# Two graph layers with residual norms on one core: the first row block of the adjacency product interleaved with making h

## What is computed

```
h  = item @ W_item.T + b_item
x1 = layernorm(x + relu(adj @ h + x @ W_user.T + b_user))
Wh = x1 @ W
e  = leaky_relu(Wh @ a[:D] + (Wh @ a[D:]).T, 0.2)
x2 = layernorm(x1 + elu(softmax(where(adj > 0, e, -9e15), axis=1) @ Wh))
```

## Time and profile before

| | |
|---|---|
| median of three runs | 2807.78 us (2807.31 to 2808.75) |
| the profiled execution, its own time | 2806.64 us |
| its span | 2804.9 us |
| TensorE (PE) busy | 2757.1 us, 98% |
| VectorE (DVE) busy | 2427.5 us, 87% |
| ScalarE (ACT) busy | 898.5 us, 32% |
| chain that ended last | PE 96%, DMA 2%, DVE 1% |
| HBM read and written | 443.85 MB and 23.55 MB |

### The profile page before, as it was taken

The page is one execution under the profiler, slowest core; times in us unless marked ns, Lnnn a source line. Parts: engine busy times, 40 slices in busy tenths (PEclk is TensorE's granted clock), DMA queues, the critical chain, the costliest instruction groups (busy, mean ns, idle before and its releaser), DMA issues.

```text
span 2804.9 us, 22893 instructions
## 1 busy us (share of the span) xinstructions
PE 2757.1 (98%) x7034; PEld 1291.7 (46%) x7034; DVE 2427.5 (87%) x2634; ACT 898.5 (32%) x730; POOL 3.5 (0%) x33
## 2 busy tenths in 40 slices
PE   7999999999999999999989999999999999999997
PEld 5444444444444444444544444444444444444454
DVE  3888888888888888888889898989898989898987
ACT  2555555555555555555550010101010101010111
POOL 0000000000000000000000000000000000000000
PEclk9999999999999999999999999999999999999999
DMA  9999999999999999999890000000000001010000
GB/s 240 326 310 324 301 312 314 311 311 312 313 313 314 310 315 310 316 308 323 257 242 0 19 15 19 16 19 15 19 16 18 27 7 34 0 34 0 16 8 14
DMA packets 309589, 468.18 MB, mean 167 GB/s; under 512 B 17176, under 2 KB 144152, under 8 KB 309400
## 3 DMA queue, kind: packets, MB, share of 16 engines
q1 hardware_dynamic: 171304, 239.32, 29.7%
q10 hardware_dynamic: 138224, 228.15, 26.8%
HBM read 443.85 MB, written 23.55 MB: 167 GB/s over the span
## 4 chain that ended last, share of the span: by engine, by line
PE 96%; DMA 2%; DVE 1%; issue 0%; ACTq 0%; ACT 0%; SPq 0%; DVEq 0%
PE bank L514 46%; PE bank L554 24%; PE bank L555 23%; DMA area_r<-in_adj_dram 1%; PE bank L512 1%; PE bank L486 1%; PE bank L542 1%; DMA area_p<-in_L_gnn_item_feat_dram 1%; DVE adj_t L598 0%; PE bank L502 0%; PE bank L462 0%; ACTq L292 0%; DMA s_scratch<-ts_row 0%; PE bank L454 0%; DMA b_user_col<-in_L_gnn_b_user_dram 0%
## 5 line engine op out<-in xcount | busy, mean ns | idle before, releaser
L514 PE MATMUL bank<-adj_t,area_h 128*128 128x512 f32 (+1 forms) x3160 | 1338.7, 583 | 1.7 <-DVE adj_t L598 1.7
L598 DVE STREAM_TRANSPOSE adj_t<-area_r 128x2048 f32<-128x2048 f32 (+3 forms) x400 | 893.1, 2233 | 198.2 <-PE bank L514 100.8
L842 DVE SCALAR_TENSOR_TENSOR adj_t<-area_r,c_col,area_h 128x1024 f32<-128x1024 uint8 (+2 forms) x790 | 953.9, 1255 | 105.6 <-PE bank L555 104.3
L514 PEld LDWEIGHTS bank<-adj_t,area_h 128*128 128x128 f32 x3160 | 597.7, 191 | 706.1 <-issue 696.9
L944 ACT ACTIVATE mask_out<-adj_t 128x4096 uint8<-128x4096 f32 (+1 forms) x200 | 700.1, 3501 | 640.0 <-DVE packing L666 371.0
L554 PE MATMUL bank<-adj_t,area_r 128*128 128x512 f32 x1580 | 808.9, 594 | 9.0 <-DVE adj_t L842 9.0
L555 PE MATMUL bank<-adj_t,area_r 128*128 128x512 f32 (+1 forms) x1580 | 776.5, 573 | 0.0
L555 PEld LDWEIGHTS bank<-adj_t,area_r 128*128 128x128 f32 x1580 | 301.4, 191 | 377.8 <-issue 377.8
L554 PEld LDWEIGHTS bank<-adj_t,area_r 128*128 128x128 f32 x1580 | 300.3, 191 | 350.6 <-issue 323.0
L775 DVE TENSOR_TENSOR area_h<-area_p,bit_of 128x2048 uint32<-128x2048 uint32 (+1 forms) x100 | 220.8, 2208 | 0.0
L1077 ACT COPY area_h<-bank 128x512 f32<-128x512 f32 x10 | 5.8, 585 | 469.3 <-PE bank L555 469.3
(11 more groups left out here) (123 smaller groups left out, 485.2 us busy)
## 6 DMA issues: line engine op xcount, KB each, us to landing
area_r<-in_adj_dram SPq DMA_DIRECT2D x312, 512.0 KB, 10.7
area_r<-in_adj_dram ACTq DMA_DIRECT2D x312, 512.0 KB, 11.0
area_r<-in_adj_dram SPq DMA_DIRECT2D x78, 480.0 KB, 8.9
area_r<-in_adj_dram ACTq DMA_DIRECT2D x78, 480.0 KB, 8.9
mask_scratch<-packed ACTq DMA_DIRECT2D x40, 320.0 KB, 9.2
area_p<-mask_scratch SPq DMA_DIRECT2D x20, 640.0 KB, 6.1
x_scratch<-area_s ACTq DMA_DIRECT2D x20, 256.0 KB, 8.3
area_h<-x_scratch SPq DMA_DIRECT2D x10, 512.0 KB, 4.0
```

The costliest lines, as they stand in the source:

```text
L514: mm = nc.tensor.matmul(acc1[par][:, 0:live], h[:, c * SPC + s, :], adj_t[:, c % 2, s * width:s * width + live], start=(c == 0 and s == 0) ...
L598: nc.vector.transpose(dst, src).then_inc(half_turned, 1)
L842: nc.vector.scalar_tensor_tensor(out=prob[:, n, 0:width], in0=lhs, scalar=c_col[:, b:b + 1], in1=unpacked[:, c % 2, n, 0:width // 4].bitca ...
```

## The change

- **Order of work.** The making of h is no longer a stage of its own. TensorE does the transposes of item chunks 0 to 2 and the products of h chunks 0 and 1, then contracts chunk 0 of block 0; behind each contraction of chunk c of block 0 it transposes item chunk c + 3 and makes h chunk c + 2. Each contraction of block 0 waits for its own chunk of h.
- **PSUM.** Item transposes use banks 4, 5 and 1, 3, the h products one pair of banks (6, 7) instead of two, so products wait for the addition of the chunk before.
- **Weights.** W_item is loaded first, with b_item, and transposed alone. W_user and W come behind the first two chunks of adjacency, and are transposed at chunk 2 of block 0, the product with the attention vectors is at chunk 3, the x transposes are at chunk 4, and the user product is at chunk 6. The setup products stand behind chunk 9, and their use on VectorE in block 1.
- **Loads.** Both queues issue in one order: item 0, item 1, the first chunk of pair 0 (`load_first`, both halves, 1 KB packets), item 2, the second chunk of pair 0, then item 3, u = 2, item 4, u = 3, item 5, u = 4. ScalarE does these before any arithmetic. Later item chunks stand on SP behind u = 6 and u = 8, on ScalarE behind the copy of each chunk.
- **Copies.** VectorE copies the transposed item chunks 0 to 2 out of PSUM, ScalarE those from 3 on, each behind the mask of chunk c - 3. The additions of h stand in VectorE's loop of block 0.

```diff
-        item_banks = (banks[4:6], banks[2:4])
-        h_banks = (banks[0:2], banks[6:8])
+        item_banks = (banks[4:6], (banks[1], banks[3]))
+        h_banks = banks[6:8]
+        ps_weights = banks[2]
...
+        def load_first(eng, part, quarters):
+            for u in range(2):
+                for a in quarters:
+                    lo = BASE[a] + part * SPC * Q
+                    src = adj[u * HG * Q:(u + 1) * HG * Q, lo:lo + SPC * Q].rearrange("(g i) w -> i g w", i=Q)
+                    eng.dma_start(raw[a * Q:(a + 1) * Q, u, :, part * SPC * Q:(part + 1) * SPC * Q], src).then_inc(first_loaded[part][u], 16)
...
         def _(sp):
+            sp.dma_start(w_in[:, 0, :], w_item).then_inc(w_item_loaded, 16)
             load_item(sp, 0, (0, 1))
-            for n, w in enumerate((w_item, w_user, w_att)):
-                sp.dma_start(w_in[:, n, :], w).then_inc(weights_loaded, 16)
...
-            for c in range(1, NC):
-                load_item(sp, c, (0, 1))
-                if c == 4:
-                    load_adjacency(sp, 0, 0, IB, (0, 1))
-                if c == 6:
-                    load_adjacency(sp, 0, 1, IB, (0, 1))
+            load_item(sp, 1, (0, 1))
+            load_first(sp, 0, (0, 1))
+            load_item(sp, 2, (0, 1))
+            load_first(sp, 1, (0, 1))
+            for n, w in ((1, w_user), (2, w_att)):
+                sp.dma_start(w_in[:, n, :], w).then_inc(weights_loaded, 16)
...
+            for u in range(2, RAW):
+                load_item(sp, u + 1, (0, 1))
+                load_adjacency(sp, 0, u, IB, (0, 1))
             load_x(0, IB)
-            for u in range(2, RAW):
+            for u in range(RAW, UPB):
                 load_adjacency(sp, 0, u, IB, (0, 1))
+                if u == 6:
+                    load_item(sp, 6, (0, 1))
+                    load_item(sp, 7, (0, 1))
+                if u == 8:
+                    load_item(sp, 8, (0, 1))
+                    load_item(sp, 9, (0, 1))
...
             pe.wait_ge(constants_made, 3)
+            pe.wait_ge(w_item_loaded, 16 * 2)
+            nc.tensor.transpose(ps_weights[:, 0:D], w_in[:, 0, :], ident).then_inc(w_item_turned, 1)
             item_transposes(0)
...
-            for c in range(NC):
-                if c + 1 < NC:
-                    item_transposes(c + 1)
-                h_products(c)
+            item_transposes(1)
+            pe.wait_ge(w_item_turned_sb, 1)
+            h_products(0)
+            item_transposes(2)
+            h_products(1)
...
                 for c in range(NC):
+                    if first:
+                        pe.wait_ge(h_ready, c + 1)
...
+                    if first:
+                        if c + 3 < NC:
+                            item_transposes(c + 3)
+                        if c + 2 < NC:
+                            h_products(c + 2)
...
+            def first_items(c):
+                dve.wait_ge(item_turned, c + 1)
+                if c == 2:
+                    dve.wait_ge(h_product, 1)
+                nc.vector.tensor_copy(item_t[:, c % 2, 0:IB], item_banks[c % 2][0][:, :])
+                nc.vector.tensor_copy(item_t[:, c % 2, IB:2 * IB], item_banks[c % 2][1][:, :]).then_inc(item_turned_dve, 1)
...
-                    if not (first and c == 0):
-                        half_transposed(k, c, 0, width)
+                    if first and c < 2:
+                        h_added(c)
+                    half_transposed(k, c, 0, width)
                     if not first or c >= 2:
                         pack2(*two)
-                    if not (first and c == 0):
-                        half_transposed(k, c, 1, width)
+                    half_transposed(k, c, 1, width)
                     if not first or c >= 2:
                         pack3(*two)
                     if not first or c >= 1:
                         pack1(*one)
                     if first and c == 1:
+                        first_items(2)
...
+                    if first and c >= 2:
+                        h_added(c)
...
+            load_item(act, 0, (2, 3))
+            load_item(act, 1, (2, 3))
+            load_first(act, 0, (2, 3))
+            load_item(act, 2, (2, 3))
+            load_first(act, 1, (2, 3))
+            for c in range(3):
+                load_item(act, c + 3, (2, 3))
+                load_adjacency(act, 0, c + 2, IB, (2, 3))
...
                     mask_chunk(k, c, width)
+                    if first:
+                        if c == 5:
+                            x_copied(k, live)
+                        if c + 3 < NC:
+                            item_copied(c + 3)
+                        if c + 6 < NC:
+                            load_item(act, c + 6, (2, 3))
```

More of the change, by code:

```diff
@@ L168, in resnorm_two_graph_layers @@
         adj_loaded = [sem(f"adj_loaded{i}") for i in range(RAW)]
+        first_loaded = [[sem(f"first_loaded{i}{u}") for u in range(2)] for i in range(2)]
         half_turned = sem("half_turned")
@@ L579, in _ @@
         def _(dve):
-            dve.wait_ge(weights_turned, 1)
-            for n in range(3):
-                last = nc.vector.tensor_copy(w_t[:, n, :], banks[n][:, 0:D])
-            last.then_inc(weights_turned_sb, 1)
-            dve.wait_ge(wa_product, 1)
-            nc.vector.tensor_copy(w_ts[:, :], banks[3][:, 0:2]).then_inc(wa_sb, 1)
+            dve.wait_ge(w_item_turned, 1)
+            nc.vector.tensor_copy(w_t[:, 0, :], ps_weights[:, 0:D]).then_inc(w_item_turned_sb, 1)
+            def first_items(c):
[4 more added lines that the diff above has]
+                nc.vector.tensor_copy(item_t[:, c % 2, IB:2 * IB], item_banks[c % 2][1][:, :]).then_inc(item_turned_dve, 1)
+            first_items(0)
+            first_items(1)
             def half_transposed(k, c, half, width):
@@ L682, in pack3, with h_added @@
                                                in1=packs[:, 5, 0:w], op0=ALU.logical_shift_left, op1=ALU.bitwise_or).then_inc(packed_to_1, 1)
-            EARLY = (6, 8)
-            for c in range(NC):
-                if c in EARLY:
-                    half_transposed(0, 0, EARLY.index(c), IB)
+            def h_added(c):
                 n = steps_of(c)
@@ L711, in transposes @@
                     if first and c == 1:
+                        first_items(2)
+                    if first and c == 3:
+                        dve.wait_ge(weights_turned, 1)
+                        nc.vector.tensor_copy(w_t[:, 1:3, :].rearrange("p n d -> p (n d)"), ps_weights[:, D:3 * D]).then_inc(weights_turned_sb, 1)
+                    if first and c == 4:
+                        dve.wait_ge(wa_product, 1)
+                        nc.vector.tensor_copy(w_ts[:, :], ps_weights[:, 3 * D:3 * D + 2]).then_inc(wa_sb, 1)
+                    if first and c >= 2:
+                        h_added(c)
+                    if isinstance(k, int) and k == 1 and c == 1:
                         dve.wait_ge(setup_products, 1)
@@ L935, in _ @@
                 last.then_inc(item_turned_sb, 1)
-            for u in range(2, RAW):
-                load_adjacency(act, 0, u, IB, (2, 3))
+            load_item(act, 0, (2, 3))
[6 more added lines that the diff above has]
+                load_adjacency(act, 0, c + 2, IB, (2, 3))
             def mask_chunk(k, c, width):
```

98 lines of the change are left out of this document (52 added, 46 removed).

## The result

The changed kernel takes **2812.48 us** (median of 20 runs, 2810.90 to 2816.32), the kernel before in the same series 2808.49 (20 runs): ratio 1.0014, 95% interval 1.0008 to 1.0020. So it is slower, clear of the noise of 20 runs but by less than the 0.2% that I had taken for what can be told. The forecast was 1.9 us slower; it is 4.0. The profiled execution took 2814.0 us with a span of 2812.2; before, 2806.64 and 2804.9.

What follows compares the result with a forecast made beforehand. TensorE was taken to bound the kernel (busy 98%), leaving only block 1's start to move: 130.3 us against 128.4, or +1.9 us on the 2807.78 median, gives 2809.7 us; range 2798 to 2818.

Steps and rivals of the forecast that it cites:

- the sum: Block 0: loads, ScalarE's queue and TensorE's remaining work added up, block 1 starting at 130.3 us against 128.4 before.
- the signs: What would show the forecast right: ScalarE's first mask at 36 to 42 us, chunk 2 at 52 to 58, block 1 at 126 to 133.
- rival 3: Loads of block 0: pairing buys no rate, 2815 us; sign under 240 GB/s between 25 and 50 us; chance 0.05.
- ScalarE held by its loads: Start of block 0: 26 loads ahead of ScalarE's first mask hold it, mask 0 done at 38.4, chunk 2 at 54.7 us.
- Rival 1: Start of block 0: ScalarE isn't held up, chunk 2 hangs on u3 alone, 2800 us; chance 0.20.
- In queues that are half a load out of step: Loads of item 3 to u3: 5.2 MB at 310 GB/s take 17 us, u3 landed at about 42 us.
- Item 6 near 62 ... Covered: SP's queue in block 0: item 6 lands near 62 us, before its transposes at about 72, so no wait.
- At chunks 3 and 5 I take 2 us each: Block 0, odd chunks: the chain of copy, issues, mask, packing and addition outlasts TensorE's work, 2 us each (0 to 4).
- The change buys the pairing of like packets: Loads of block 0: both queues in the same order, so like packets meet; 365 GB/s for two full queues of 2 KB packets.
- rival 2: Block 0: ScalarE's queue stays full throughout, 4 us each at chunks 3 and 5, slower loads, 2816 us; chance 0.20.

Runs made afterwards that it cites:

- e1: The changed kernel with item 6 loaded on SyncE's queue ahead of u5 instead of behind u6: 2809.39 us, 1.0008 to the kernel before.
- e10: e5 with the b_item load moved from SyncE's to ScalarE's queue: 2805.01 us, 0.9991 to the kernel before.
- e5: The changed kernel with W_user, W and the three short vectors loaded behind x and used two chunks later: 2817.84 us, 1.0035 to the kernel before.
- e2: The changed kernel with the three short vectors loaded behind u3, the attention product waiting on their own semaphore: 2817.39 us, 1.0035 to the kernel before.
- e4: The kernel before with every adjacency load issued on SyncE's queue, none by ScalarE: 3282.89 us (one run).

## Why the prediction was right, and where its steps were not

Sign and place came out, and the size within 2.8 us: 2812.48 against 2809.7, the whole of it ahead of block 1. The number is better than the working, and part of that is luck. Block 1 started at 135.77 where the sum has 130.3 and the signs 126 to 133; of these 5.5 us the medians show 2.8, since the trace is of a run 1.5 us above its median. And 2812.48 lies as near to rival 3 (2815) as to the forecast. By its steps:

- **ScalarE held by its loads: right.** Mask 0 ended at 38.9 (38.4), the products of chunk 2 at 44.7 (44.0), mask 1 at 49.5 (50.6), chunk 2 at 56.0 (54.7). Rival 1 (not held, 2800) is out.
- **"In queues that are half a load out of step": failed.** SyncE's queue was 4.4 loads behind. That is 0.4 from a whole period, so the rate taken came out all the same, by luck: 311 GB/s from 30 to 48 us for the 310. What failed is the time of the small loads: 208 GB/s from 24 to 30 us, 288 over 25 to 50, and u3's second half at 49.5 for 42. It cost only 1.3 us at chunk 2, because mask 1 was as late. I had counted the small loads by bytes, and they are next to none; they count by packets.
- **"Item 6 near 62 ... Covered": failed**, and it is the largest error. It landed at 78.89, with 6.11 us of wait and 2.3 of half clock: 8.4 us. I had u6 landing at 60 with both queues full; but SyncE's was behind, and x and the vectors stood ahead of it.
- **"At chunks 3 and 5 I take 2 us each": failed** the other way. In the timeline of TensorE no line from 56 to 78 and none from 84 to 135 us has a wait. The four issues took 2.75 us at 64.90, and mask 3 was done at 71.4, before the transposes of item 6 could begin; what it was late by lay under that wait. In e1, without that wait, the products behind chunk 3 follow their transposes at once (76.32), so the 2 us weren't there either.
- The sum with these three put right: 130.3 + 1.3 - 4.0 + 8.4 = 136.0; measured 135.77. So 9.7 us that I had left out and 4 us too many partly cancelled.
- **"The change buys the pairing of like packets": right**, and the changed kernel has most of it, though only because its lag happens to be near a whole period: its order is the same in both queues, its position isn't. Rival 3 (pairing buys no rate, 2815) gave nearly the right time for a wrong reason: its own sign, and e10 against e5, speak against it. Of rival 2 the full queue shows ahead of mask 1 alone.

What stays open: why ScalarE's queue gets 136 to 192 packets ahead early on, and how much of the time from 60 to 100 us (236 to 278 GB/s in all kernels of the new order) is due to phase and how much to queues run dry. Neither was tried by itself.

## What to carry to other kernels

When two queues feed one core in packets of 512 B and 2 KB, count packets and not bytes, and keep the two level, or a whole period apart, so that like sizes meet; check it by the packets that each queue has started, since the count by the program alone was off by a third to two thirds of a load here. A small load took a turn of its queue for each packet, so put it where nothing urgent stands behind, and look at the phase that it leaves: moving small loads back without that cost 5 us (e2, e5). Sharing them out over both queues early on wasn't tried. And if a stage isn't bound by its engine, removing its waits one by one moves them on to the next load; ask for the bytes by the time that the engine can take them first.

## What the runs showed of the hardware that I hadn't expected

- While both queues are full they start equal numbers of packets (3202 and 3201 in 24 to 48 us of the changed kernel, 489 and 489 in 54 to 59 us of e5), even 4 B against 2 KB.
- A pair of packets takes 169 ns with 2 KB and 2 KB, 164 with 2 KB and 512 B, 65 with 512 B and 512 B. Beside a packet of 2 KB one of 512 B costs as much as another of 2 KB. One load of 64 KB moved from one queue to the other was worth 12.8 us.
- One queue alone took 150 ns a packet (641 in 50 to 56 us) or 131 (85469 in 300 to 1000 us of e4), so the second queue's packet adds 19 to 38 ns to it.
- One full queue nearly alone reached 224 GB/s with the DMA engines 103.7% busy (e4); with a second one beside it 365 (60 to 72 us).
